# The first expert of a layer: its tokens turned ahead of the expert loop, piece by piece

## The chip, the cores and the metric

The kernel runs on one core of one Trainium2 chip. The metric is device time in microseconds (us), from the start of the program to its end, of one launch that computes the whole block. Three runs of the kernel before are known; the median is 1078.22 us.

The engines are named as the profile names them: PE is TensorE (PEld its weight loads, PEldq its sequencer, which takes waits, branches and register work and hands the rest on), DVE is VectorE, ACT is ScalarE, POOL is GpSimd, SP is SyncE.

## What is computed

A block of three parts over 2048 tokens of 512 features: half a mixture of experts, a gated linear mixer with a short convolution, and the mixture again.

```
x = x + 0.5 * moe(layernorm(x))      # layer 0 of the experts
x = x + mixer(layernorm(x))
x = x + 0.5 * moe(layernorm(x))      # layer 1, the same weights

moe: top1 = argmax(tokens @ gate.T); each of 8 experts takes its first 320 tokens
     hmid = gelu(dispatch[e] @ wi[e])       # 512 -> 2048
     eout = hmid @ wo[e]                    # 2048 -> 512
     out[token] = softmax probability * eout
```

## The kernel before, in words

All is float32. A product is made of three PE products of a high and a low part (`product`, L1253 to L1255), so for each weight block ACT rounds a high part and DVE takes the difference to it (L805), for weights and tokens alike.

**Routing.** At the start of each mixture PE computes the gate's logits and ranks, and at last a table of source rows, row statistics and weights by expert (`tabulate`, L1388). DVE turns the table into row indices (L938, L940) and packs, for each expert, a code of three bits for its width class into one register word (`pack_counts`, `taken_done`). The classes are 192, 240, 272, 288, 304 and 320 token columns.

**The first expert's tokens.** POOL gathers its rows from memory in three pieces of 128 rows (`gather`, L490). ACT normalises each piece as it lands, into `dn` (L639), and increments `dn_done` by one for each. PE turns the pieces, so that features lie on partitions: 128 x 128 transposes of `dn` into four PSUM banks, one for each 128 features (`TURNED`, `turn_tokens`, L1442). When a bank has its three pieces `tokT_done` rises; ACT takes the high part of it (L629) and DVE the low part (L805, `dt_lo`). The first product of an expert waits for all four.

**The expert loop on PE.** `for e in 0..7` (L1531): two register operations take the expert's width class from the word; a branch (L1535) goes to a narrow part (two pieces) or a wide part (three pieces). Each turns the tokens of expert e, then transposes the result of expert e - 1 (`turn_out`, L1485, eight transposes; for e = 0 there is no result and nobody reads what they write), then tests the width class by class (`dispatch`, L1523, L1525) and jumps to the body written for that width (`run_288_0` is the body of width 288 in layer 0). A body first waits for the third bank (`dt_lo`), clears the accumulators (L1448), does the last four transposes of the previous result (`turn_rest`, L1492), and then loops four times over `mm1`, `mm1`, `mm2`, `mm2`.

**Blocks of code and visits.** `addr_align(256, ...)` places pieces of PE's program on multiples of 256 instructions. The loop head stands at the start of such a block, and so do the first bodies. Behind the first bodies (two in layer 0, six in layer 1: `VISITED`) stands a visit: two instructions that only jump back. Ahead of the loop `peek` jumps to the next visit and returns (L1400; the visit's own instructions are L1553 and L1554); a prefetch hint for the next visit (L1404) stands where the last one returned. In layer 0 both visits lie between the table and the loop, in layer 1 the last three of six.

Counted from the program, the body of width 272 in layer 0 starts a block and has 104 multiplications, each a weight load and a matmul, and 16 other instructions, so 224 of 256. The body of width 288 follows it without alignment: its first 19 instructions come before its loop, which begins at place 243 of the block and goes on in the next one.

Of the kernel before, what the change touches and what calls it, by code (L numbers as in the profile page):

```python
# [28 lines left out]
P = 128  # L29
# [3 lines left out]
DC = D // P  # L33
# [3 lines left out]
CHUNKS = 3  # L37
# [3 lines left out]
NARROW = 2  # L41
# [17 lines left out]
NW = len(WIDTHS)  # L59
# [30 lines left out]
def build_kernel(nc, x, wuT, wvT, wg1T, wg2T, small_in, wi, wo, out):  # L90
# [6 lines left out]
    with ExitStack() as ctx:  # L97
# [3 lines left out]
        def at(name, shape, dt, offset):  # L101
            return nc.alloc_sbuf_tensor_at(name, shape, dt, offset=offset)
# [7 lines left out]
        def put(name, shape, dt):  # L110
            t = at(name, shape, dt, top[0])
            top[0] += size(shape, dt)
            return t
# [10 lines left out]
        ident = put("ident", [P, P], F32)  # L124
# [24 lines left out]
        code = put("code", [P, 1], I32)  # L149
# [30 lines left out]
        dn = at("dn", [P, CHUNKS, D], F32, a_xn)  # L180
# [146 lines left out]
        TURNED = (acc[0], acc[1], psH[1], psH[0])  # L327
# [111 lines left out]
        def _(pool):  # L439
# [55 lines left out]
            for n, s in enumerate(layers):  # L495
# [25 lines left out]
                def expert(e, a, more, s=s, source=source, target=target):  # L521
                    for i, (k, _) in enumerate(HELD):
                        m = ROWS[k]
                        pool.wait_ge(s.out_dve, 3 + 3 * e + i + 1)
                        if not isinstance(e, int):
                            pool.sem_inc(may_send, 1)
                        pool.indirect_dma_start(target[:, :],  # L527
                                                bass.IndirectOffsetOnAxis(ap=dst_now[0:m, a, k:k + 1], axis=0),
                                                rows[a][0:m, k, :], None).then_inc(s.res_out, 16)
                    if more:  # L530
                        pool.wait_ge(s.res_out, 48 * e + 48)
                        gather(e + 2, a, source, s)
# [716 lines left out]
        def _(pe):  # L1249
# [28 lines left out]
            codes = pe.alloc_register("codes")  # L1278
            width = pe.alloc_register("width")
# [21 lines left out]
            for n, s in enumerate(layers):  # L1301
# [77 lines left out]
                def tabulate(first, end, s=s, n=n):  # L1379

                    for t in range(first, end):
                        if t % LT == 0:
                            pe.wait_ge(s.lanes_done, t // LT + 1)
                        if t % LT == 0 and t < HALF_B[n]:
                            pe.wait_ge(s.facts_pool, t // LT + 1)
                        if t == HALF_B[n]:
                            pe.wait_ge(s.facts_dve, 1)
                        ins = pe.matmul(psH[0][:, 0:Q * FACTS], at_lane[:, t, :],  # L1388
                                        at_facts[:, t].rearrange("p f q -> p (f q)"),
                                        start=(t == 0), stop=(t == TILES - 1))  # L1390
                    if end == TILES:
                        ins.then_inc(s.tabled, 1)

                def peek(n=n):

                    done = visits[n]
                    if done:
                        w = PLACED[len(done) - 1]
                        done[-1] = nc.cur_bb
                        pe.br(f"visit_{w}_{n}").branch_hint(marks.pop())  # L1400
                        nc.switch_bb(f"visited_{w}_{n}", parent=done[-1])
                    if len(done) < VISITED[n]:
                        done.append(None)
                        marks.append(pe.mark_branch_hint_location())  # L1404
# [23 lines left out]
                if n == 0:  # L1428
                    warm(WARM_LANES)
                tabulate(SPLIT[n], TILES)  # L1430
                for _ in range(3):
                    peek()

                def turn_tokens(e, chunks, s=s):

                    pe.wait_ge(s.dn_done, CHUNKS * e + CHUNKS)
                    for c in range(DC):
                        if c < 2:
                            pe.wait_ge(s.eoT_sum, DC * e + c + 1)
                        for k in range(chunks):  # L1440
                            q = k * P
                            ins = pe.transpose(TURNED[c][:, q:q + P], dn[:, k, c * P:(c + 1) * P], ident[:, :])  # L1442
                        ins.then_inc(s.tokT_done, 1)
# [34 lines left out]
                def turn_out(e, s=s):  # L1478

                    pe.wait_ge(s.out_dve, 3 * e)  # L1480
                    for c in range(DC):
                        pe.wait_ge(s.eoT_sum, DC * e + c + 1)
                        for k, bank in HELD[1:]:
                            q, m = k * P, ROWS[k]
                            pe.transpose(bank[0:m, c * P:(c + 1) * P], eoT[:, c, q:q + m], ident[:, :])  # L1485
# [30 lines left out]
                def dispatch(what, ks, n=n):  # L1516

                    pe.br(f"{what}_test_{ks[0]}_{n}")
                    for k in ks:
                        w = WIDTHS[k]  # L1520
                        with nc.body(f"{what}_test_{k}_{n}", valid_engines=[pe.engine]):
                            if k < ks[-1]:
                                pe.br_lt(width, k + 1, on_true=f"run_{w}_{n}", on_false=f"{what}_test_{k + 1}_{n}")  # L1523
                            else:
                                pe.br(f"run_{w}_{n}")  # L1525

                pe.wait_ge(s.taken_done, 1)
                pe.reg_load(codes, code[0:1, 0:1])
                pe.wait_ge(s.wi_lo, 1)
                pe.addr_align(BLOCK, offset=BLOCK - 2, max_nops=0)  # L1530
                with pe.Fori(0, E) as e:  # L1531
                    pe.reg_alu(width, codes, 2 ** CODE - 1, ALU.bitwise_and)
                    pe.reg_alu(codes, codes, CODE, ALU.logical_shift_right)
                    head = nc.cur_bb
                    pe.br_lt(width, NARROW, on_true=f"narrow_{n}", on_false=f"wide_{n}")  # L1535
                    for what, chunks, ks in (("narrow", CHUNKS - 1, range(NARROW)), ("wide", CHUNKS, range(NARROW, NW))):
                        with nc.body(f"{what}_{n}", parent=head, valid_engines=[pe.engine]):
                            turn_tokens(e, chunks)
                            turn_out(e)
                            dispatch(what, ks)  # L1540
                    nc.switch_bb(f"join_{n}", parent=head)
# [184 lines left out]
```

## Time and profile before

| | |
|---|---|
| median of 3 runs | 1078.22 us (1077.0 to 1085.58) |
| the profiled execution | 1078.21 us, span 1076.5 us |
| PE busy | 1030.2 us, 96% of the span |
| PE's mean granted clock | 0.982 |
| first expert of layer 0, width 288 | first product at 44.83 us |
| first expert of layer 1, width 320 | first product at 674.61 us |

Times in the trace count from the start of the span. A row of the timeline gives start, duration, engine, line, operation, tiles, shape, number merged, and in brackets the idle time before it and what ended it. `PEclk` is the share of the clock that PE was granted: 1.00 is 2.4 GHz and 0.50 is 1.2 GHz.

### The profile page before, as it was taken

To read this page: it belongs to the slowest core of one execution; us is meant where nothing else is said; L and a number is where in the kernel's file an instruction comes from. 1 tells how busy PE (TensorE), PEld (TensorE's weight loads), DVE (VectorE), ACT (ScalarE), POOL (GpSimd) and SP (SyncE) were. 2 spreads that over 40 slices of the span, in tenths; PEclk is the share of its full clock that TensorE was granted. 3 is DMA by queue.
4 is the path that set the end of the run, shared out by engine and by line. 5 is a ranking of instruction groups with operands and counts; after the bars stand their busy time and mean duration, and the time that the engine had idled before them with its cause. 6 is when DMAs were issued, how large, how long until landed. Compare 5 with 4: busy or idle time off the path is not lost.

```text
span 1076.5 us, 20121 instructions
## 1 busy us (share of the span) xinstructions
PE 1030.2 (96%) x7380; PEld 964.0 (90%) x7380; DVE 748.5 (70%) x1174; ACT 543.2 (50%) x851; POOL 136.6 (13%) x142
## 2 busy tenths in 40 slices
PE   9699999999999999699999996999999999999997
PEld 6699999999999999568787775999999999999997
DVE  8566666777677778468777765557788788775653
ACT  5445454655456566254333223455656666654442
POOL 3201111112020210100000013002021131120101
PEclk9899999999999999899999998999999999999999
DMA  8388646476556653220010144446565765754420
GB/s 314 107 305 286 217 136 230 149 256 214 184 189 218 222 173 116 74 107 1 1 40 1 40 159 140 157 156 205 201 248 182 260 214 204 269 207 165 138 82 25
DMA packets 83278, 177.34 MB, mean 165 GB/s; under 512 B 4192, under 2 KB 4704, under 8 KB 83168
## 3 DMA queue, kind: packets, MB, share of 16 engines
q1 hardware_dynamic: 75488, 152.61, 40.8%
q0 software_dynamic: 7168, 23.07, 6.3%
q10 hardware_dynamic: 576, 1.05, 0.3%
q8 instruction: 28, 0.46, 0.2%
q14 instruction: 18, 0.15, 0.0%
HBM read 162.04 MB, written 18.87 MB: 168 GB/s over the span
## 4 chain that ended last, share of the span: by engine, by line
PE 85%; DVE 6%; issue 3%; ACT 2%; DMA 2%; POOL 1%; DVEq 0%; ACTq 0%; SPq 0%; POOLq 0%
PE psH L1253 13%; PE psH L1255 13%; PE acc L1265 13%; PE psH L1254 13%; PE acc L1266 11%; PE acc L1261 9%; PE acc L1253 3%; PE acc L1255 3%; PE acc L1254 3%; DVE dtl L805 1%; DVE row_stats L838 1%; PE psH L1492 1%; PE psT L1589 1%; ACT eoT L689 1%; PE psT L1317 1%
## 5 line engine op out<-in xcount | busy, mean ns | idle before, releaser
L1253 PE MATMUL psH<-dth,wih 128*128 128x240 f32 (+5 forms) x1024 | 295.3, 288 | 0.1
L1255 PE MATMUL psH<-dth,wil 128*128 128x240 f32 (+5 forms) x1024 | 293.6, 287 | 0.0
L1254 PE MATMUL psH<-dtl,wih 128*128 128x240 f32 (+5 forms) x1024 | 293.3, 286 | 0.0
L1266 PE MATMUL acc<-ht,wol 128*128 128x240 f32 (+5 forms) x1024 | 286.4, 280 | 0.0
L805 DVE TENSOR_TENSOR wol<-raw_wo,woh 128x1024 fp32r<-128x1024 f32 x128 | 155.5, 1221 | 106.9 <-ACT woh L622 106.7
L1265 PE MATMUL acc<-ht,woh 128*128 128x320 f32 (+3 forms) x1024 | 210.5, 299 | 0.0
L656 ACT ACTIVATE gel<-psH 128x320 f32<-128x320 f32 x256 | 111.9, 437 | 188.7 <-PE psH L1255 181.5
L622 ACT ACTIVATE woh<-raw_wo 128x1024 fp32r<-128x1024 f32 x128 | 134.6, 1059 | 123.0 <-PE acc L1266 123.0
L1253 PEld LDWEIGHTS psH<-dth,wih 128*128 128x128 f32 x1024 | 193.5, 189 | 1.5 <-ACT gel L656 0.8
L1254 PEld LDWEIGHTS psH<-dtl,wih 128*128 128x128 f32 x1024 | 193.6, 189 | 0.0
L1266 PEld LDWEIGHTS acc<-ht,wol 128*128 128x128 f32 x1024 | 193.6, 189 | 0.0
L1255 PEld LDWEIGHTS psH<-dth,wil 128*128 128x128 f32 x1024 | 193.6, 189 | 0.0
L1265 PEld LDWEIGHTS acc<-ht,woh 128*128 128x128 f32 x1024 | 166.1, 188 | 0.0
L1261 PE MATMUL acc<-ht,woh 128*128 128x480 f32 (+1 forms) x512 | 159.7, 372 | 0.2 <-DVE ht L805 0.2
L805 DVE TENSOR_TENSOR wil<-raw_wi,wih 128x1024 fp32r<-128x1024 f32 x128 | 154.6, 1218 | 0.1
L611 ACT ACTIVATE wih<-raw_wi 128x1024 fp32r<-128x1024 f32 x128 | 134.6, 1053 | 0.0
L1050 DVE CAST ht<-gel 128x640 fp32r<-128x640 f32 x128 | 64.3, 502 | 95.7 <-ACT gel L656 95.2
L805 DVE TENSOR_TENSOR ht<-gel,ht 128x640 fp32r<-128x640 f32 x128 | 105.7, 826 | 4.4
L1261 PEld LDWEIGHTS acc<-ht,woh 128*128 128x128 f32 x512 | 96.1, 188 | 7.6 <-DVE ht L805 0.6
L527 POOL DMA_INDIRECT x<-rows,dst_now x24 | 28.9, 1204 | 325.0 <-DVE rows L1106 322.3
L527 POOL DMA_INDIRECT out_x<-rows,dst_now x24 | 29.5, 1227 | 310.9 <-DVE rows L1106 308.1
L639 ACT ACTIVATE dn<-rows,facts_now 128x512 f32<-128x512 f32 x48 | 37.3, 807 | 43.7 <-DVE facts_now L1030 28.6
(200 smaller groups left out, 1174.7 us busy)
## 6 DMA issues: line engine op xcount, KB each, us to landing
raw_wi<-in_wi SPq DMA_DIRECT2D x64, 1024.0 KB
raw_wo<-in_wo SPq DMA_DIRECT2D x64, 1024.0 KB, 5.5
out_x<-xt SPq DMA_DIRECT2D x4, 1024.0 KB, 5.8
xt<-in_x SPq DMA_DIRECT2D x6, 512.0 KB, 8.3
xt<-x SPq DMA_DIRECT2D x3, 1024.0 KB, 10.4
raw_u<-in_wuT SPq DMA_DIRECT2D x1, 1024.0 KB
raw_u<-in_wvT SPq DMA_DIRECT2D x1, 1024.0 KB
xt<-in_x ACTq DMA_DIRECT2D x2, 256.0 KB, 3.8
```

What stands on the lines that cost most here:

```text
L527: pool.indirect_dma_start(target[:, :], bass.IndirectOffsetOnAxis(ap=dst_now[0:m, a, k:k + 1], axis=0), rows[a][0:m, k, :], None).then_inc ...
L611: act.activation(wih[:, step % 2, :, :], raw_wi[k][:, :, (step % 2) * HALF:(step % 2 + 1) * HALF], copy).then_inc(s.wi_hi, 1)
L622: act.activation(woh[:, step % 2, :, :], raw_wo[k][:, (step % 2) * ICS:(step % 2 + 1) * ICS, :], copy).then_inc(s.wo_hi, 1)
L656: act.activation(gel[:, step % 2, j, :], psH[j][:, 0:CAP], ACT.Gelu).then_inc(s.gelu_done, 1)
L805: return dve.tensor_tensor(out, full, hi.bitcast(F32), ALU.subtract)
L1050: dve.tensor_copy(hth[:, k, :, :], gel[:, k, :, :]).then_inc(s.ht_hi, 1)
L1253: pe.matmul(out, lh, rh, start=first, stop=False)
L1254: pe.matmul(out, lh, rl, start=False, stop=False)
L1255: return pe.matmul(out, ll, rh, start=False, stop=last)
L1261: pe.matmul(bank.rearrange("p (r q) -> p r q", r=2)[:, :, 0:w], lh, both[:, :, 0:w], start=False, stop=False, skip_group_check=True)
L1265: pe.matmul(bank[:, 0:w], lh, both[:, r, 0:w], start=False, stop=False, skip_group_check=True)
L1266: return pe.matmul(bank[:, 0:w], ll, both[:, 0, 0:w], start=False, stop=False, skip_group_check=True)
```

## The change

PE turns the first expert's tokens ahead of the loop. Piece k of all four banks is turned as soon as `dn_done` reaches k + 1. The wait for `taken_done` and the load of the code word move ahead of piece 0, and the last visit of the layer stands behind piece 0. In the loop the first instruction after the register work is a new branch on the loop counter: for e = 0 it goes to a chain of its own with all six width tests, and no token and no result is transposed there; for the other seven experts it goes to a second branch, the one on the width that stood there before.

```diff
                 tabulate(SPLIT[n], TILES)
-                for _ in range(3):
-                    peek()
+                peek()
+                peek()
+
+                def turn_piece(k, s=s):
+
+                    pe.wait_ge(s.dn_done, k + 1)
+                    q = k * P
+                    for c in range(DC):
+                        ins = pe.transpose(TURNED[c][:, q:q + P], dn[:, k, c * P:(c + 1) * P], ident[:, :])
+                        if k == CHUNKS - 1:
+                            ins.then_inc(s.tokT_done, 1)
+
+                pe.wait_ge(s.taken_done, 1)
+                pe.reg_load(codes, code[0:1, 0:1])
+                turn_piece(0)
+                peek()
+                for k in range(1, CHUNKS):
+                    turn_piece(k)
...
-                pe.wait_ge(s.taken_done, 1)
-                pe.reg_load(codes, code[0:1, 0:1])
                 pe.wait_ge(s.wi_lo, 1)
                 pe.addr_align(BLOCK, offset=BLOCK - 2, max_nops=0)
                 with pe.Fori(0, E) as e:
                     pe.reg_alu(width, codes, 2 ** CODE - 1, ALU.bitwise_and)
                     pe.reg_alu(codes, codes, CODE, ALU.logical_shift_right)
                     head = nc.cur_bb
-                    pe.br_lt(width, NARROW, on_true=f"narrow_{n}", on_false=f"wide_{n}")
+                    pe.br_lt(e, 1, on_true=f"first_{n}", on_false=f"later_{n}")
+                    with nc.body(f"first_{n}", parent=head, valid_engines=[pe.engine]):
+                        dispatch("first", range(NW))
+                    with nc.body(f"later_{n}", parent=head, valid_engines=[pe.engine]):
+                        pe.br_lt(width, NARROW, on_true=f"narrow_{n}", on_false=f"wide_{n}")
```

PE in layer 0, between the table and the loop, before. `L1400` is the jump to a visit, `L1528` the load of the code word, `L1535` the branch on the width, `L1442` the turning of tokens inside the loop:

```order
L1404 BRANCH_PREFETCH_HINT
L1400 UNCONDITIONAL_BRANCH
L1528 TENSOR_LOAD code
L1530 ISA
L1531 UNCONDITIONAL_BRANCH
L1532 REGISTER_ALU
L1533 REGISTER_ALU
L1535 COMPARE_AND_BRANCH
```

The same place now. The hint for the last visit still stands where the visit before it returned; between it and its jump (`L1400`) stand now the load and the first piece (`L1439`):

```order
L1404 BRANCH_PREFETCH_HINT
L1444 TENSOR_LOAD code
L1439 MATMUL acc<-ident,dn 128x128 x2
L1439 MATMUL psH<-ident,dn 128x128 x2
L1400 UNCONDITIONAL_BRANCH
L1439 MATMUL acc<-ident,dn 128x128 x2
L1439 MATMUL psH<-ident,dn 128x128 x2
L1439 MATMUL acc<-ident,dn 128x128 x2
L1439 MATMUL psH<-ident,dn 128x128 x2
```

Then the loop's head, where the new tests (`L1539`, `L1541`) come in front of the narrow part. The eight transposes of `turn_out` are `L1501` now, and the first expert no longer passes them:

```order
L1549 COMPARE_AND_BRANCH
L1534 UNCONDITIONAL_BRANCH
L1539 COMPARE_AND_BRANCH x5
L1541 UNCONDITIONAL_BRANCH
L1553 COMPARE_AND_BRANCH
L1452 ISA
L1455 ISA
L1458 MATMUL acc<-ident,dn 128x128 x2
```

The turning of the first expert moved from the loop to a place ahead of it, and each later expert passes one compare-and-branch more. The bodies keep their places in the blocks, since the blocks in front of them are aligned as before.

## Rows read from the trace of the kernel before

**Rows 1.** The page: busy time by engine, and the chain that ended last.

```profile
PE 1030.2 (96%) x7380; PEld 964.0 (90%) x7380; DVE 748.5 (70%) x1174; ACT 543.2 (50%) x851; POOL 136.6 (13%) x142
...
PE 85%; DVE 6%; issue 3%; ACT 2%; DMA 2%; POOL 1%; DVEq 0%; ACTq 0%; SPq 0%; POOLq 0%
```

**Rows 2.** Timeline of the first expert's start in layer 0.

```profile
34.72 0.81 ACT L639 ACTIVATE dn<-rows,facts_now 128x512 f32<-128x512 f32 x1 [6.24 <-DMA rows<-in_x,src_now]
...
37.49 1.69 ACT L639 ACTIVATE dn<-rows,facts_now 128x512 f32<-128x512 f32 x2 [1.96 <-DMA rows<-in_x,src_now]
...
39.66 1.54 PE L1442 MATMUL acc<-ident,dn 128*128 128x128 f32 x6 [9.04 <-ACT dn L639]
40.60 0.44 ACT L629 ACTIVATE dth<-acc 128x320 fp32r<-128x320 f32 x1 [1.42 <-PE acc L1442]
...
42.27 1.92 PE L1485 MATMUL psT<-ident,eoT 128*128 128x128 f32 x8
42.35 1.13 DVE L805 TENSOR_TENSOR dtl<-psH,dth 128x320 fp32r<-128x320 f32 x2
...
43.98 0.29 PE L1448 MATMUL acc<-nil,ones 128*128 128x2 bf16 x4
...
44.83 0.59 PE L1253 MATMUL psH<-dth,wih 128*128 128x288 f32 x1
```

**Rows 3.** Timeline of the first expert's start in layer 1.

```profile
668.36 1.52 ACT L639 ACTIVATE dn<-rows,facts_now 128x512 f32<-128x512 f32 x2 [1.29 <-DMA rows<-out_x,src_now]
...
670.59 1.54 PE L1442 MATMUL acc<-ident,dn 128*128 128x128 f32 x6 [9.24 <-ACT dn L639]
...
673.20 1.11 PE L1485 MATMUL psT<-ident,eoT 128*128 128x128 f32 x8
...
674.61 0.39 PE L1253 MATMUL psH<-dth,wih 128*128 128x320 f32 x1
```

**Rows 4.** Timeline of the second expert's start in layer 0.

```profile
96.22 0.76 ACT L629 ACTIVATE dth<-acc 128x320 fp32r<-128x320 f32 x2
...
98.14 0.25 PE L1448 MATMUL acc<-nil,ones 128*128 128x2 bf16 x4
```

**Rows 5.** Granted clock by stretch: stretch, its length, busy us of each engine, PEclk, DMA share, GB/s.

```profile
36.00:38.00 2.00, 0.00 (x0) 0.00 (x0) 0.00 (x0) 0.51 (x1) 0.00 (x0) 0.50 0.52 139
...
45.00:45.40 0.40, 0.40 (x4) 0.40 (x4) 0.16 (x1) 0.00 (x0) 0.00 (x0) 0.64 0.58 215
...
673.00:673.50 0.50, 0.50 (x5) 0.50 (x5) 0.35 (x2) 0.30 (x2) 0.50 (x1) 0.66 1.13 426
```

**Rows 6.** PE's sequencer by line: min/median/max ns, first and last start; visits of both layers.

```profile
L1400 PEldq COMPARE_BRANCH  x1: 3195/3195/3195, 34.1 to 34.1; - x1
...
L1400 PEldq COMPARE_BRANCH  x5: 312/388/2407, 641.0 to 661.3; - x5
```

**Rows 7.** PE's sequencer by line, layer 0, from the loop's entry to the first products.

```profile
L1530 PEldq COMPARE_BRANCH  x1: 170/170/170, 38.4 to 38.4; - x1
...
L1523 PEldq COMPARE_BRANCH  x2: 82/264/447, 40.2 to 40.4; - x2
...
L1507 PEldq FUSED_REGOPS  x1: 37/37/37, 40.9 to 40.9; - x1
...
L1454 PEldq ALU_OP  x1: 32/32/32, 45.6 to 45.6; - x1
```

**Rows 8.** DMA queue of PE's code: the whole span, then from 43.0 to 44.2 us.

```profile
q8 instruction: 28, 0.46, 0.2%
...
q8 instruction: 1, 0.02, 5.7%
```

**Rows 9.** A start of a later expert: its width branch, sequencer and first weight load.

```profile
L1535 PEldq COMPARE_BRANCH  x15: 77/77/446, 94.7 to 1007.4; - x15
...
L1439 PEldq FUSED_REGOPS  x1: 37/37/37, 202.2 to 202.2; - x1
...
202.68 0.37 PEld L1442 LDWEIGHTS acc<-ident,dn 128*128 128x128 f32 x3
```

## The prediction

> **What bounds the kernel now.** I read the page first: PE is busy 96% of the span and makes 85% of the chain that ended last [rows 1]. Outside the change's places PE's order stays as it is, so what counts is when its first product of each layer starts and at which clock. Then the timeline of the two places where PE stands idle ahead of an expert. It waits 9.04 us in layer 0 and 9.24 us in layer 1, until ACT has normalised the third piece [rows 2, 3]. Piece 0 is ready at 34.72 + 0.81 = 35.53, pieces 1 and 2 at 38.3 and 37.49 + 1.69 = 39.18; in layer 1 the last is ready at 668.36 + 1.52 = 669.88. Behind that stand 12 transposes (8 in a narrow expert), 8 more whose output nobody reads, the clearing and the first product at 44.83 and 674.61: 5.65 and 4.73 us from the last piece to the first product. Third, the granted clock: 0.50 while PE idles; it returns inside 45.0 to 45.4 (a mean of 0.64 puts it at 45.29) and inside 673.0 to 673.5 (0.66: 673.34) [rows 5]. Last, the sequencer and the code queue [rows 6 to 8], since the change also moves a visit and adds tests.
>
> **Pieces turned ahead.** At half clock the first transposes step by about 0.21 us (six in 1.54 us, less one of about 0.47, over five) [rows 2]. ACT's first copy could start only when a bank had three, 40.60 - 39.66 = 0.94 after the first. With piece 2 alone left, one transpose is enough: 39.18, plus 0.05 for the semaphore, plus 0.94 - 2 x 0.21 = 0.52, gives a first copy at 39.75 instead of 40.60. From the first copy to the clearing an undisturbed start takes 98.14 - 96.22 = 1.92 us [rows 4], so clearing at 41.65. Before it came at 43.98, because the 8 unread transposes filled 1.92 us of PE [rows 2]; they are gone. From clearing to the first product take the half-clock 44.83 - 43.98 = 0.85: the first product of layer 0 starts at 42.5, **2.3 us earlier**. Layer 1: 669.88 + 0.05 + 0.52 = 670.45, + 1.92 = 672.37; the sequencer has more to pass there (below), I take 672.5, + 0.85 = 673.35: **1.25 us earlier**. So far the change would save 3.6 us. ACT and DVE have nothing else at that time: DVE's last low part moves with the copies, and the splits of `wo` behind them just start earlier.
>
> **The visit behind piece 0.** The visit was 3.20 us long in layer 0, from 34.1 to 37.3, almost all of it waiting for code; in layer 1, where the hint had stood long before the jump, the jumps took 0.31 us at least and 0.39 in the middle of five [rows 6]. So the hint itself starts the fetch. The hint keeps its time, and the load (0.4 us) and piece 0 (35.53 to 35.75) fit in before the code is there at 37.3. The visit costs nothing, and pieces 1 and 2 come later anyway (38.3, 39.18). Bounds: nothing, or a full 3.2 us behind piece 0 (a rival).
>
> **The tests.** From the jump into the loop (38.4) to the body (40.9) the sequencer took 2.5 us [rows 7], about 1.1 of it ahead of the wait for pieces. Now all of it comes after piece 2: from 39.25, some 1.1 us, the new branch and jump (about 0.5), three tests not passed and one taken (0.6): about 41.4, just ahead of the clearing at 41.65; in layer 1 with width 320, two tests more, 672.5. That is the term I used. The seven later experts of each layer pass one compare-and-branch more, taken: I price it from the row of the old one, 0.08 not taken and up to 0.27 with the jump. At the shortest of the 14 starts the sequencer was ready for the transposes at 202.22 and PE took the first weights at 202.68 [rows 9]: 0.46 us of cover, so 0. Without that cover, 14 x 0.27 = 3.8 us.
>
> **Code blocks.** The code queue moved 28 packets, 0.46 MB, so about 16 KB each [rows 8], and I take one for a block of 256 instructions, since the kernel aligns to that. The Trainium skill says the same (Runtime: NRT & Kernel Launch, Instruction fetch mechanics: 16 KiB blocks of 256 instructions). Layer 0's body of width 288 has its loop from place 243, so 13 instructions of it, three or four register ones and five products, lie in one block and the rest in the next. Nobody visited that one. Its packet moves inside 43.0 to 44.2 [rows 8], not before, though the sequencer had entered the block ahead at 40.9 [rows 7]: the DMA engines are full there. The sequencer then gets through its first twelve products only at 45.6 [rows 7], 2.7 us after it entered that loop. PE saw nothing of this, because the fifth product was due at 45.5 anyway. Now the first product starts at 42.5, the fifth is done by about 44, and the sixth must wait for the block. It entered the block ahead at 40.9 and will now at 41.4, so the packet is no earlier: the sixth product comes at 45.65 at best and at 46.2 if the packet slips with the entry, where it was at 45.8. **The 2.3 us of layer 0 are gone**: between -0.1 and +0.4. Layer 1's bodies start blocks, and each fits in one; nothing of this there.
>
> The skill speaks against this price: on the same page it calls the crossing of a block boundary "mostly hidden". By that the 2.3 us stay, which is the first rival below.
>
> **The clock.** The full level came 45.29 - 39.66 = 5.6 us after the first transpose of an unbroken run in layer 0 and 673.34 - 670.59 = 2.75 us in layer 1. The change breaks that run: the 8 unread transposes kept PE at work while ACT and DVE split the tokens. Now, in layer 1, PE idles from about 670.9 to 672.5, the run starts at 672.5 and the clock returns between 675.2 and 678.1. Products run at half pace until then: (675.2 - 673.35) / 2 = 0.9 to 2.4 us lost against 1.25 won, so -0.3 to +1.1, and I take **+0.3**. In layer 0 PE idles again from 44 to 45.8, so the clock returns 2.75 to 5.6 us after 45.75: 1.4 to 2.8 us lost, where before the clock was full from the third product on. With the block's -0.1 to +0.4 that is +1.3 to +3.1, and I take **+1.7**, nearer the case where the clock returns at the first chance, as in layer 1.
>
> The Trainium skill (TensorE: Matmul & The Clock Gate, Part 4) says that transposes do not count as work for the full clock. Here the clock returned at 673.34 with only transposes behind it since 670.59, so the measurement decides against the sentence for these float32 transposes; by the sentence the dropped ones cost nothing and layer 1 would gain its 1.25 us.
>
> **Sum.** 1078.21 + 1.7 + 0.3 = **1080.2 us**, against the profiled execution, which agrees with the median (1078.22). PE is the bound from there to the end of each layer, so nothing behind absorbs it. Own range of this case: +1.0 to +4.2, 1079.2 to 1082.4. A program of this kind can be told from no change at about 1%, 11 us; all cases here lie far within.
>
> **The rivals.**
> - *The pieces pay off* (chance 0.3). The block is fetched in time in layer 0 and the clock returns about when it did. Then layer 0 wins 2.3 us of start and runs its products from 42.5 to 45.29 at half pace, 1.4 lost against 0.2 before: -1.1. Layer 1 wins up to 1.25: 1075.8 with both, 1077.7 if the clock is later. For it: sequential fetching works everywhere in the trace without a visible stop of PE. Against it: the packet that moves only after 43.0 with the engines full. It decides at the sixth product of layer 0: at or before 44.2 it is this case.
> - *The visit falls behind piece 0* (0.08). If the hint does not start the fetch, the visit runs 35.75 to 39.0 or 39.6, eight transposes follow (1.7 us), the first copy is at about 40.8 instead of 40.60 and, in layer 1, at 671.3 + 0.9 + 0.5 = 672.7 instead of 671.5. The change then doesn't do what it says, and both layers pay for the clock: +4 us, 1082.
> - *The extra branch per expert shows* (0.06): cover of 0.46 us is thin. +3.8 on the forecast, 1084; with the first rival, 1080.
> - Forecast 0.5; 0.06 for what I don't see.
>
> **Numbers.** Likeliest 1080.2. From the first rival's lower end with a little for a measurement's scatter to the visit's and part of the branch's, 1075.2 to 1083.6. Faster by over 1%: 0.02. Within 1%: 0.95. Slower by over 1%: 0.03, for a stall of code in every expert that no row shows.
>
> **What would show it.** In the profile after: transposes of piece 0 at about 35.6, of piece 2 right behind ACT's last piece; ACT's first copy at 39.75 and clearing at 41.65; first product at 42.5. Then the deciding rows: an idle gap of PE of 1.5 to 2 us behind the fifth product of layer 0, and PEclk of 0.50 up to 48.5 or later; in layer 1 no such gap, and PEclk of 0.50 up to 675.2 or later. No idle time ahead of the transposes of the other 14 experts. It is wrong if the sixth product follows the fifth at once, if the clock is back at 45.3 and 673.3, or if the second visit's jump in layer 0 ends after 37.5.

## The result: 6.6 us slower, where 2.0 were forecast

| | before | after |
|---|---|---|
| median of 20 runs each, us | 1079.34 | 1085.95 |
| lowest and highest, us | 1076.45, 1085.58 | 1083.34, 1089.03 |
| profiled execution, us | 1078.21 | 1088.86 |
| its span, us | 1076.5 | 1087.0 |

The ratio is 1.006, with a 95% interval of 1.0048 to 1.0073. So the change costs 0.6%. The forecast of 1080.2 us had the direction; the measured median lies above the top of its range, 1083.6.

**Where the time went, by the two traces.** I measure each layer's start from the end of the last matmul of the table (L1388), because what lies ahead of it has the same work in both kernels and its own scatter. The end of the stretch is ACT's first copy of tokens for the second expert. After, in layer 0, these rows of the timelines give 102.28 - 34.39 = 67.9, and in layer 1 741.85 - 667.40 = 74.45 (start, length, engine, line, operation; the third column from the end is the number of instructions):

```profile
34.00 0.39 PE L1388 MATMUL psH<-at_facts,at_lane 128*128 128x96 f32 x2
...
102.28 0.76 ACT L629 ACTIVATE dth<-acc 128x320 fp32r<-128x320 f32 x2
...
667.01 0.39 PE L1388 MATMUL psH<-at_facts,at_lane 128*128 128x96 f32 x2
...
741.85 0.76 ACT L629 ACTIVATE dth<-acc 128x320 fp32r<-128x320 f32 x2
```

The same rows of before give 96.22 [rows 4] - 30.62 = 65.6 and 731.55 - 661.35 = 70.2:

```profile
30.23 0.39 PE L1388 MATMUL psH<-at_facts,at_lane 128*128 128x96 f32 x2
...
660.85 0.50 PE L1388 MATMUL psH<-at_facts,at_lane 128*128 128x96 f32 x3
...
731.55 0.76 ACT L629 ACTIVATE dth<-acc 128x320 fp32r<-128x320 f32 x2
```

So **layer 0 lost 2.3 us and layer 1 lost 4.25**, 6.5 together, nearly all of the 6.6 us between the medians. The two spans differ by 10.5; 3.8 of that is the table of layer 0 ending later (34.39 against 30.62), and it isn't the change: among the experiments below that contain the change, whose work up to that point is the same, the one profiled execution ends the table at 34.1 to 34.4 in e2 and e6 and at 30.5 to 31.3 in e3, e5, e7, e9 and e10.

**Layer 0.** After, PE's timeline:

```profile
39.46 0.69 PE L1439 MATMUL acc<-ident,dn 128*128 128x128 f32 x2 [5.08 <-ACT dn L639]
...
41.57 0.69 PE L1439 MATMUL acc<-ident,dn 128*128 128x128 f32 x2 [0.99 <-ACT dn L639]
...
42.76 0.69 PE L1439 MATMUL acc<-ident,dn 128*128 128x128 f32 x2
...
45.09 0.27 PE L1464 MATMUL acc<-nil,ones 128*128 128x2 bf16 x4 [1.21 <-DVE dtl L805]
...
45.91 0.59 PE L1253 MATMUL psH<-dth,wih 128*128 128x288 f32 x1
...
47.25 0.44 PE L1255 MATMUL psH<-dth,wil 128*128 128x288 f32 x1
49.57 0.61 PE L1253 MATMUL psH<-dth,wih 128*128 128x288 f32 x1 [1.87 <-issue]
```

The three pieces are turned as ACT delivers them, and the first product starts 45.91 - 34.39 = 11.5 us behind the table; before it was 44.83 - 30.62 = 14.2 [rows 2]. The start is 2.7 us earlier. Then, behind the sixth product, PE idles for 1.87 us that the view puts down to "issue", which is PE's own sequencer. The code queue between 46.9 and 48.3 moved one packet, with the software queue at 77.7% of all engines beside it (queue: packets, MB, share of 16 engines):

```profile
q0 software_dynamic: 115, 0.36, 77.7%
q8 instruction: 1, 0.02, 5.3%
```

The seventh product starts 49.57 - 34.39 = 15.2 behind the table, before at 15.3: the start won is gone. On top of it the clock is 0.50 until 54.7, which is 20.3 behind the table; before it was full from 45.29, which is 14.7 behind (stretch, length, busy us of each engine, PEclk, DMA share, GB/s; compare [rows 5]):

```profile
37.64:54.50 16.86, 10.88 (x46) 9.23 (x47) 3.50 (x6) 6.39 (x11) 4.25 (x4) 0.50 0.44 149
54.50:55.00 0.50, 0.50 (x4) 0.50 (x4) 0.14 (x1) 0.50 (x2) 0.00 (x0) 0.80 0.00 0
```

**Layer 1.** The waits of PE from 672 to 690 us of after (line, what it waited for: us in total, times, longest), and the timeline there:

```profile
PE acc L1439 <- ACT dn L639: 6.6, 2, 5.4
PE acc L1464 <- issue: 6.0, 1, 6.0
```

```profile
671.98 0.81 ACT L639 ACTIVATE dn<-rows,facts_now 128x512 f32<-128x512 f32 x1 [5.26 <-DMA rows<-out_x,src_now]
...
676.41 0.64 PE L1439 MATMUL psH<-ident,dn 128*128 128x128 f32 x2
...
677.72 0.88 DVE L805 TENSOR_TENSOR dtl<-psH,dth 128x320 fp32r<-128x320 f32 x2
...
683.07 0.27 PE L1464 MATMUL acc<-nil,ones 128*128 128x2 bf16 x4 [6.02 <-issue]
...
683.89 0.62 PE L1253 MATMUL psH<-dth,wih 128*128 128x320 f32 x1
```

The last piece is turned by 677.05 and DVE is done with the tokens at 678.60, but PE clears only at 683.07. Its sequencer is what is late. These are its rows at the loop's entry (register moves ahead of the loop, and the first instruction of the loop's body):

```profile
L1545 PEldq MOVE  x2: 34/36/38, 676.3 to 676.4; - x2
...
L1546 PEldq ALU_OP  x1: 36/36/36, 681.8 to 681.8; - x1
```

Between the two there is nothing but a block boundary, since the kernel aligns the loop's head to a block (L1544), and **the sequencer stood there for 5.3 us**. Before, it passed the same boundary in 0.2 us, and only then came to the wait for the pieces:

```profile
L1531 PEldq MOVE  x2: 34/36/38, 669.3 to 669.4; - x2
...
L1532 PEldq ALU_OP  x1: 36/36/36, 669.7 to 669.7; - x1
```

After, a code packet moves in that time, at 679.0 to 680.2 (the queues from 678.9 to 680.3, the software queue again at 77%):

```profile
q0 software_dynamic: 120, 0.43, 76.8%
q1 hardware_dynamic: 80, 0.13, 24.6%
q8 instruction: 1, 0.02, 5.4%
```

Over the whole span the code queue moved 29 packets after, 28 before [rows 8].

### The profile page after: what moved, and what is told of

Read it like the earlier page. It is cut to its first block, busy times and chain, and to the rows that moved or that the text cites. A ratio compares the mean times of both kernels' runs of the same rounds, so it can differ in the third digit from the quotient of the medians.

```text
span 1087.0 us, 20095 instructions
## 1 busy us (share of the span) xinstructions
PE 1036.6 (95%) x7364; PEld 967.7 (89%) x7364; DVE 747.2 (69%) x1174; ACT 542.9 (50%) x851; POOL 135.6 (12%) x142
## 4 chain that ended last, share of the span: by engine, by line
PE 85%; DVE 5%; issue 4%; ACT 3%; DMA 2%; POOL 1%; DVEq 0%; ACTq 0%; SPq 0%; POOLq 0%
PE psH L1253 13%; PE acc L1265 13%; PE psH L1255 13%; PE psH L1254 13%; PE acc L1266 11%; PE acc L1261 9%; PE acc L1253 3%; PE acc L1255 3%; PE acc L1254 3%; DVE dtl L805 2%; PE psT L1317 1%; PE psH L1508 1%; PE psT L1607 1%; ACT eoT L689 1%; PE acc L1334 1%
## 6 DMA issues: line engine op xcount, KB each, us to landing
raw_u<-in_wuT SPq DMA_DIRECT2D x1, 1024.0 KB, 10.2
```

## The experiments

"L0" and "L1" are the stretch from the table to the second expert in each layer, as above, in one profiled execution each. "Clock back" is the time behind the table at which the full clock returned. The same code of a layer can differ by up to 1.8 us from one execution to another (L0 of e7, e9 and e10: 63.3, 64.9 and 65.1), and L1 of e1 is 1.0 us longer than that of before, with a third piece 0.4 us later. So smaller differences of L0 and L1 show nothing by themselves. The ratio and its interval are estimated from all runs, and the ratio isn't the quotient of the two medians.

| kernel | median, us | ratio to before (95%) | L0 | L1 | clock back L0, L1 |
|---|---|---|---|---|---|
| before | 1079.34 | | 65.6 | 70.2 | 14.7, 12.0 |
| after | 1085.95 | 1.006 (1.0048 to 1.0073) | 67.9 | 74.45 | 20.3, 18.8 |
| e1 branch alone | 1080.42 | 1.0004 (0.999 to 1.0018) | 64.8 | 71.2 | 12.5, 14.4 |
| e2 visits first | 1086.97 | 1.0061 (1.004 to 1.0082) | 67.25 | 74.6 | 19.8, 19.0 |
| e3 body 288 elsewhere | 1087.48 | 1.0076 (1.0053 to 1.0098) | 64.2 | 74.6 | 14.6, 18.9 |
| e4 no unread transposes | 1079.65 | 1.0014 (0.9996 to 1.0032) | 64.8 | 69.5 | 13.1, 11.4 |
| e5 pieces in the loop head's block | 1080.62 | 1.0009 (0.9991 to 1.0026) | 67.0 | 70.0 | 18.6, 14.6 |
| e6 e5, bodies placed | 1080.85 | 1.0004 (0.9987 to 1.0022) | 65.1 | 70.1 | 16.8, 15.0 |
| e7 e6, PE kept at work | 1079.55 | 0.9993 (0.9974 to 1.0011) | 63.3 | 71.3 | never fell, 10.0 |
| e8 before, PE kept at work | 1079.44 | 0.9997 (0.9979 to 1.0015) | 66.8 | 70.1 | 19.0, 0.6 |
| e9 e7 in layer 0 alone | 1078.78 | 0.999 (0.9976 to 1.0004) | 64.9 | 70.8 | 8.1, 15.1 |
| e10 e9, 4 matmuls behind in layer 1 | 1076.39 | 0.9969 (0.9951 to 0.9987) | 65.1 | 68.2 | 9.5, 10.7 |

Each experiment was measured beside before again; its median there was 1079.79 with e1 to e4, 1079.96 with e5 to e8, and 1079.53 with e9 and e10.

**e1: the branch alone.** Before, with the branch on the counter and a path of its own for the first expert that does just what the wide path did.

```diff
-                    pe.br_lt(width, NARROW, on_true=f"narrow_{n}", on_false=f"wide_{n}")
+                    pe.br_lt(e, 1, on_true=f"first_{n}", on_false=f"later_{n}")
+                    with nc.body(f"first_{n}", ...):
+                        turn_tokens(e, CHUNKS)
+                        turn_out(e)
+                        dispatch("first", range(NW))
+                    with nc.body(f"later_{n}", ...):
+                        pe.br_lt(width, NARROW, on_true=f"narrow_{n}", on_false=f"wide_{n}")
```

> The kernel before with the branch on the loop counter alone: the first expert has a path of its own in the loop, but turns its tokens there and does the unread transposes as before. Theory (code blocks and clock): the branch costs nothing, all later experts have at least 0.46 us of cover: ratio to before 0.999 to 1.001, and no idle PE of over 1 us at either loop entry. Rival (the branch itself is what costs): +4 us or more, ratio 1.004 or more, and the 5 us stop of the sequencer in layer 1 between the loop's register moves and the first register operation is there too.

Measured: no difference, and the later experts take what they took (55.95, 51.17 and 45.5 us for the second to fourth of layer 0 in both). The branch costs nothing that shows, in the 14 later experts either (the ratio's interval leaves room for 1.9 us). The 6.6 us belong to the rest of the change.

**e2: the visits out of the way.** After, with all visits ahead of the load and the pieces.

```diff
                 peek()
+                peek()
...
-                turn_piece(0)
-                peek()
-                for k in range(1, CHUNKS):
+                for k in range(CHUNKS):
```

> The changed kernel with all visits ahead of piece 0, as before the change; the pieces still ahead of the loop. Theory (the loop head's block is pushed out while the sequencer waits for the pieces in the block ahead of it): the 5.3 us stop in layer 1 stays, ratio to before 1.005 to 1.007. Rival (the visit amid the pieces is what does it): the stop is gone, about 4 us less than the change, ratio 1.001 to 1.003.

Measured: nothing recovered in the time; L1 is 74.6 as in after, and the sequencer stops for 5.35 us at the same boundary. It is not the visit amid the pieces that costs.

**e3: the body of width 288 at the start of a block.** After, with the bodies in another order.

```diff
-PLACED = (240, 192, 272, 288, 304, 320)
+PLACED = (240, 192, 288, 272, 304, 320)
```

> The changed kernel with the bodies of widths 272 and 288 exchanged in the program, so that layer 0's first expert (288) has a body that starts a block and fits in it, in the block that is fetched behind the last visit. Theory: the 1.9 us gap of PE behind the sixth product of layer 0 is gone, the clock comes back some 3.4 us earlier, layer 1 unchanged with its 5.3 us stop: 1.9 to 3.5 us less than the change, ratio to before 1.003 to 1.005. Rival (the gap comes from something else, a wait of mm1): the gap stays and the ratio is 1.006 as for the change.

Measured: the gap behind the sixth product is gone (seventh product 13.3 behind the table instead of 15.2, L0 3.7 us shorter), so the gap was the block that nobody had fetched. But the theory had the ratio fall to 1.003 to 1.005, and it was 1.0076. The second expert, of width 304, now had a gap of the same size in the midst of its products; its rows in e3:

```profile
100.18 0.30 PE L1255 MATMUL psH<-dth,wil 128*128 128x304 f32 x1
102.41 0.30 PE L1253 MATMUL psH<-dth,wih 128*128 128x304 f32 x1 [1.92 <-issue]
...
103.38 0.46 PE L1254 MATMUL psH<-dtl,wih 128*128 128x304 f32 x1
```

and with it its own fall of the clock (0.30 us a product becomes 0.46 us from 103.38 to 106.67): this expert took 59.59 us instead of 55.95. So the 3.7 us won in the first expert were lost again in the second. e6 places both bodies so that they are fetched ahead.

**e4: the unread transposes.** Before, with e1's branch, whose first path leaves out the eight transposes that nobody reads.

```diff
+                    with nc.body(f"first_{n}", ...):
+                        turn_tokens(e, CHUNKS)
+                        dispatch("first", range(NW))
```

> The kernel before with the branch on the loop counter and a first path that leaves out the eight unread transposes; tokens turned inside the loop as before. Theory (they kept PE at work and the clock came back sooner): first products about 1.2 us earlier in both layers, but the clock back later by 0 to 3.4 us, in layer 0 again a wait for the next block: ratio 1.000 to 1.002. Rival (transposes do not count for the clock): the clock is back as long after the first product as before, 1 to 2.5 us won: ratio 0.998 to 0.999.

Measured: 64.8 and 69.5, 0.7 us less than before in each layer, and no difference in the median. The first products come 1.7 and 0.7 us earlier; in layer 0 PE then idles 0.6 us behind the sixth product. The clock did not come back later, as the theory had it, but 1.6 and 0.6 us earlier than before, so that against the first product it stayed within 0.15 us of where it was, as the rival said. One execution each doesn't settle it: e1, which has all these transposes, has its clock back 2.2 us earlier than before in layer 0 and 2.4 later in layer 1. This half of the change shows no cost; what costs is where the pieces are turned.

**e5: pieces and loop head in one block.** After, with the alignment in front of piece 0 instead of in front of the loop.

```diff
                 pe.reg_load(codes, code[0:1, 0:1])
+                pe.addr_align(BLOCK, offset=BLOCK - 1, max_nops=0)
                 turn_piece(0)
...
                 pe.wait_ge(s.wi_lo, 1)
-                pe.addr_align(BLOCK, offset=BLOCK - 2, max_nops=0)
                 with pe.Fori(0, E) as e:
```

> The changed kernel with one alignment moved: the block of the loop head now begins in front of piece 0, so the sequencer waits for the pieces inside it and crosses no block between the pieces and the loop. Theory (the block behind the one it waits in is lost once the packet after the last visit has landed): the 5.3 us stop of layer 1 is gone, first product there about 11.5 us after the table instead of 16.5; layer 0 keeps its gap; table to the second expert's tokens in layer 1 about 69.5 to 71 us instead of 74.5; ratio to before 1.001 to 1.003. Rival (the stop belongs to the new branch or to the tests, wherever they stand): the stop stays, 1.006.

Measured: the stop of layer 1 is gone, and with it 4.4 us of L1 and most of the change's cost. The waits of PE from 668 to 690 us in e5, where after had 6.0 us of issue:

```profile
PE acc L1439 <- ACT dn L639: 6.7, 2, 5.7
PE acc L1465 <- DVE dtl L805: 1.2, 1, 1.2
```

Layer 0 keeps its gap (1.2 us, L0 67.0), as it should, since its body of width 288 lies where it lay.

**e6: both effects mended.** e5, with the bodies of the two widths that layer 0 meets first (288 and 304) placed first, so that the two visits of layer 0 fetch them.

```diff
-PLACED = (240, 192, 272, 288, 304, 320)
+PLACED = (288, 304, 240, 272, 192, 320)
```

> The same, with the bodies placed 288, 304, 240, 272, 192, 320, so that layer 0 visits just the bodies of its first two experts and each lies in a block of its own. Theory: neither the gap behind the sixth product (1.9 us and the clock) nor a stop at the second expert; layer 0 from table to the second expert's tokens about 64.2 us instead of 67.9, second expert 55.9; ratio 0.998 to 1.001. Rival (the second expert or a later one now pays for a body not fetched, as the exchange of 272 and 288 did with 3.6 us): ratio 1.001 or more.

Measured: no gap in either expert (the second takes 55.96 us), L0 65.1, L1 70.1, and the median of before. Its products of layer 0 start 11.5 us behind the table like after's, 2.7 earlier than before's, and follow one another without a gap. Yet only 0.5 us is left at the second expert, since they run at half pace until 16.8 instead of 14.7. The rest of the start went to the clock:

```profile
45.86 0.59 PE L1253 MATMUL psH<-dth,wih 128*128 128x288 f32 x1
...
47.21 0.44 PE L1255 MATMUL psH<-dth,wil 128*128 128x288 f32 x1
47.45 0.44 PE L1253 MATMUL psH<-dth,wih 128*128 128x288 f32 x1
```

**e7: PE kept at work.** e6, with matmuls on constants (128x512, bf16, output unread) wherever PE would wait: 12 ahead of the visits, 6 ahead of and 8 behind piece 0, 2 ahead of pieces 1 and 2, 8 behind the last.

```diff
+                warm(12)
                 peek()
...
+                warm(6)
                 turn_piece(0)
+                warm(8)
                 peek()
                 for k in range(1, CHUNKS):
+                    warm(2)
                     turn_piece(k)
+                warm(8)
```

> The same, and PE kept at work with matmuls of ones into a free bank (12 ahead of the visits, 6 and 8 around piece 0, 2 ahead of pieces 1 and 2, 8 behind them). Theory (the clock is what is left): the granted clock does not fall ahead of the first expert, or returns before its first product; another 1.5 to 3 us in each layer; ratio 0.993 to 0.997, below both kernels. Rival (the extra matmuls stand in the way of visits and pieces): no gain over the kernel without them.

Measured: in layer 0 the clock was never 0.50 ahead of the products, and L0 is 63.3, the shortest of all:

```profile
42.87 0.38 PE L1253 MATMUL psH<-dth,wih 128*128 128x288 f32 x1
43.09 0.29 PE L1254 MATMUL psH<-dtl,wih 128*128 128x288 f32 x1
```

In layer 1 it lost 1.1: a visit took 3.99 us there, the matmuls stood in front of the pieces, and the first copy of tokens came 12.0 us behind the table instead of 10.2. The third piece itself was ready 1.1 us later than before. The median doesn't tell it from before, so the forecast of 0.993 to 0.997 missed.

**e8: the same without the change.** Before, with matmuls on constants.

```diff
-                for _ in range(3):
-                    peek()
+                warm(12)
+                peek()
+                peek()
+                warm(12)
+                peek()
...
+                warm(8)
```

> The kernel before, nothing turned ahead, with the matmuls of ones alone (12 ahead of the first visit, 12 ahead of the last, 8 behind it). Theory: transposes and the unread ones run at the full clock, first products 1.5 to 2.5 us earlier in each layer; ratio 0.996 to 0.998. It tells how much of the gain of the kernel before this one is the clock's alone. Rival: the same time as before.

Measured: the first product of layer 0 comes 11.3 us behind the table, at full clock, in a kernel that turns nothing ahead. Then the missing block stops it for longer than in after:

```profile
42.77 0.29 PE L1255 MATMUL psH<-dth,wil 128*128 128x288 f32 x1
45.55 0.40 PE L1253 MATMUL psH<-dth,wih 128*128 128x288 f32 x1 [2.49 <-issue]
```

So with the bodies where they lie, an earlier start of layer 0 runs into that block also where it isn't made by turning pieces ahead. The clock, full until then, fell in the first products behind this gap (at 46.3) and was back at 49.75, which is the 19.0 of the table. In layer 1 nothing was won (70.1), and the ratio missed the forecast of 0.996 to 0.998.

**e9 and e10: less of it.** e9 is e7 with the matmuls on constants in layer 0 alone; e10 adds four in layer 1, behind the last piece.

```diff
-                warm(12)
+                if n == 0:
+                    warm(12)
...
-                warm(8)
+                warm(8 if n == 0 else 4)
```

> The layout of e6 (pieces and loop head in one block, widths of the first experts placed as in e6), with the matmuls on constants of e7 in layer 0 alone; layer 1 is e6's. Theory (two code stops and the clock account for everything): layer 0 goes from the table to the second expert in about 63.3 us, as in e7, against 65.6 before; layer 1 in about 70.1, as in e6; so 2.4 us less than before, ratio 0.998. Rival (the matmuls on constants cost in layer 1 because the pieces are turned late, whatever the matmuls do): layer 1 near 71.3 again and a ratio of 1.000.

> As e9, with four matmuls on constants in layer 1 as well, behind the last piece alone, where the eight unread transposes stood before the change. Theory: PE's run is not broken there, so the clock returns nearer to 12.0 us behind the table, as before, instead of 15.0 as in e6, and the second expert of layer 1 comes 0.5 to 1.5 us earlier than e6's 70.07: about 69.1, ratio 0.997. Rival (they only hold up the first product): layer 1 at 70.5 or later and nothing won over e9.

Measured: e10 is the fastest kernel of the study and the only one whose interval lies below 1: 0.9969 (0.9951 to 0.9987), 3.1 us less than before. It is one of ten kernels tried, so some luck may be in it; but its median is also 2.4 us below that of e9, from which it differs by the four matmuls alone. Its one profiled execution is the slowest of its ten (1079.65) and took 3.6 us more than before in the mixer between the two mixtures, which no edit here touches; so the trace is read here for layer 1 alone. That layer did as expected and more: PE's run isn't broken behind the last piece, the products are at full pace from the second on, and L1 is 68.2 where e9 and e6 have 70.8 and 70.1. Its timeline, and the windows of its clock:

```profile
674.25 1.73 PE L1286 MATMUL psT<-ones 128*128 128x512 bf16 x4
675.82 0.24 PE L1474 MATMUL acc<-nil,ones 128*128 128x2 bf16 x4
...
676.28 0.39 PE L1253 MATMUL psH<-dth,wih 128*128 128x320 f32 x1
676.51 0.31 PE L1254 MATMUL psH<-dtl,wih 128*128 128x320 f32 x1
```

```profile
668.00:675.60 7.60, 4.49 (x16) 2.74 (x16) 2.06 (x5) 4.19 (x8) 3.05 (x4) 0.50 0.56 162
675.60:676.10 0.50, 0.50 (x8) 0.38 (x7) 0.40 (x2) 0.50 (x2) 0.20 (x2) 0.93 1.03 389
```

Layer 0 missed: 64.9 and 65.1 instead of 63.3. In e9 the clock fell to 0.50 at 35.26, and the six matmuls ahead of piece 0 took 2.69 us instead of 1.46; in e10 it fell at 37.38, as piece 0 was turned, and the ten behind it took 3.58 us instead of 2.32. So the pieces came late (first copy 11.4 and 11.6 us behind the table instead of 9.8). The same code kept the clock once and lost it twice, and e7's 63.3 was the better of the cases seen. The rival of e9 got its ratio nearly right (0.999) but not for its reason: there are no matmuls on constants in its layer 1, and its 70.8 goes with a third piece that was normalised 1.1 us later than in after.

## Why the prediction was wrong

Step by step, in the order in which it was made.

- **Pieces turned ahead**: right. The first product of layer 0 came 2.7 us earlier (forecast 2.3). The forecast took the idle time before the pieces as ended by ACT alone; in fact before's sequencer came to its wait only at 39.57 and 670.49, 0.4 and 0.6 us after the last piece was ready, and this went as well. Layer 1's 1.25 can be read in e5, where nothing stops: 674.48 - 662.70 = 11.8 behind the table against 674.61 - 661.35 = 13.3 [rows 3], 1.5 earlier.
- **The visit behind piece 0**: right, it costs nothing. Its jump took 996 ns, from 39.5, in the row below; piece 1 was turned at 41.57, at once behind ACT's 41.51. e2 says the same.

```profile
L1400 PEldq COMPARE_BRANCH  x2: 996/2263/3530, 33.4 to 39.5; - x2
```

- **The tests**: right. In layer 0 they ended at 44.65 and the clearing waited for DVE until 45.09.
- **Code blocks of layer 0**: right in kind and size. The forecast had the waiting product at 45.65 to 46.2, which is 15.0 to 15.6 behind the table; it came at 15.2. It was the seventh and not the sixth, so the loop's part in the first block holds one product more than I counted; by its letter the sign "wrong if the sixth product follows the fifth at once" came true, though what it was to tell, that no block is missing, did not. The rival that had the block in time is out. With the block there, in e3 and e6, L0 is 1.4 and 0.5 us less than before, where the rival had 1.1. The Trainium skill's "mostly hidden" for a block's boundary (Runtime: NRT & Kernel Launch, Instruction fetch mechanics) holds for most boundaries of this trace (the loop head's is passed 16 times in after, 15 of them in 0.3 us or less) and not for these two, 1.87 and 5.3 us.
- **The clock in layer 0**: the mechanism right, the size small. I took +1.7 for the layer, near the earliest return; the clock came back 5.1 us after the seventh product, towards the latest, and the layer cost +2.3, inside the +1.3 to +3.1 given.
- **The clock in layer 1**: the number right, by e5: L1 70.0 against 70.2, -0.2 in place of +0.3 (from -0.3 to +1.1). The reason is less sure. The clock was back 14.6, 15.0 and 15.1 behind the table in e5, e6 and e9, where the run is broken, against 12.0 before; but e1, where it is unbroken, has 14.4, and e4, without the unread transposes, 11.4.
- **The step that failed** is the sentence "Layer 1's bodies start blocks, and each fits in one; nothing of this there." It looks at the bodies alone and so puts a fetch at the loop's head at nothing. Before, the sequencer passed that boundary without a stop (669.45 to 669.69) and only then came to the wait for the pieces. Now the pieces stand in the block ahead of the head, the boundary is passed behind the last of them, the head's code is not there at that time, and every microsecond of its fetch holds up the start: 5.3 us. Layer 1 measured +4.25 where the sum had +0.3. With e5's layer 1 and after's layer 0 the sum would be +2.1, and the forecast was +2.0; that they agree so well is in part luck, since e5 itself has +1.4 in layer 0, and its median is 0.7 us above before's.

I had priced "a stall of code" only as a chance of 0.03 in every expert. The range's upper end held the visit's full price and part of the branch's, both of which turned out to be nothing, and nothing for the head of a loop.

**What stays open** is why layer 1 had to fetch the head at all. The same instructions in layer 0, where two visits lie ahead and not six, pass the same boundary at 43.2 to 43.5 without a stop:

```profile
L1545 PEldq MOVE  x2: 38/40/42, 43.1 to 43.2; - x2
...
L1546 PEldq ALU_OP  x1: 42/42/42, 43.5 to 43.5; - x1
```

In layer 1 a code packet had ended at 675.8, before the sequencer reached the boundary at 676.45, and yet another one had to come. e2 and e3 have the same order, with 1.0 and 0.8 us between the two, and stop as well. In before, e1 and e4 the sequencer passes the boundary ahead of that packet's end (669.69 at the latest against 670.28 in before), and none of them stops. So it looks as if the packet behind the last visit pushes the head's block out while the sequencer still waits in the block ahead, which is the theory that e5 was made for. What fits with it is room: in after, e2 and e3 a second code packet moves in the second expert of layer 1 (745.1 in after), and that expert, whose body (width 240) was the first to be visited, takes 46.3 to 46.5 us instead of 45.5, as if its code too had been lost. But e4 has that second packet as well (734.3, and 46.6 us) without any stop at the head, so the one loss doesn't tell of the other. The Trainium skill describes PE's instruction memory as a FIFO of 128 KiB filled in blocks of 16 KiB (the same section). By an estimate from that it holds eight, as many as six bodies, the block of the pieces and the head take up, so that one more would push one out. No run here counts them; one with fewer visits in layer 1 would be the test, and wasn't made.

## What to carry to other kernels

Work that is moved ahead of a loop also moves the passage into the loop's code behind it: if the engine waits in the block before the head, a fetch of the head can come behind the wait, as it did in layer 1 and not in layer 0. With the waiting instructions and the head in one block (e5) there was no such fetch. A start that comes earlier is worth only what the next block of code and the clock leave of it; look for the next instruction whose code nobody has fetched before the gain is counted, and in the second expert too, since a gap mended in one place came back whole in the next. Matmuls of no use can be worth their time where they keep PE at work just ahead of the products: four of them behind the last piece went with a start of layer 1 1.9 us shorter than e6's and a median 2.4 us below e9's. Many of them, in front of pieces and visits, won nothing (e7, e8), and leaving out the eight unread transposes cost nothing (e4).

## What the runs showed of the hardware

- The sequencer's stop at a block boundary was 5.3 us, where a jump to a body whose code had to be fetched took 3.5 us at most in that kernel. Beside the software queue's transfers, at 77% of the engines, a code packet of 16 KB took 1.2 us; 2.5 us of the stop pass before the packet starts (676.45 to 678.98) and 1.6 us behind its end.
- In layer 0 PE resumed 1.4 us after the packet had ended (46.98 + 1.20 = 48.18, product at 49.57), so the packet's end isn't the moment from which its code runs.
- A branch on the loop counter showed no cost in 14 starts of an expert, the shortest of which had 0.46 us of cover [rows 9].
- The granted clock can fall or stay in the same code: with the same matmuls on constants in layer 0 it never fell in e7, and it fell in e9 and e10 and was back 8.1 and 9.5 us behind the table, with an L0 1.6 and 1.8 us longer.
